# A two-layer decoder on one core: block-diagonal attention keys written by 16 loads per unit instead of a load and a multiplication by a mask of heads

## The chip, the cores and the metric

The kernel runs on one core of one Trainium2 chip. A core has TensorE (PE: matrix products), VectorE (DVE), ScalarE (ACT), GpSimd (POOL) and SyncE (SP), which here only issues DMA transfers. Each engine works through its own list of instructions in order; engines wait for each other by counting semaphores. The metric is the time of one execution on the device, in microseconds (us).

## What is computed

The input x has 16 batches of 512 positions of 256 numbers; the context has 16 batches of 64 positions. Six sublayers follow each other, each on a layer norm of x and added to x. Those the change touches are the two cross attentions (16 heads of 16 numbers, 64 keys):

```python
x = x + L0_attn(_layernorm(x), ...)       # gated recurrence along the positions
x = x + L0_xattn(_layernorm(x), ctx, ctx, mask, ...)
x = x + L0_ffn(_layernorm(x), ...)
x = x + L1_attn(_layernorm(x), ...)       # an LSTM of 20 units gives positions of attention
x = x + L1_xattn(_layernorm(x), ctx, ctx, fside, mask, ...)
x = x + L1_ffn(_layernorm(x), ...)        # one of 8 experts per position
...
Q = q @ Wq.T + bq; K = k @ Wk.T + bk; V = v @ Wv.T + bv      # each split into 16 heads
scores = einsum('bhqd,bhkd->bhqk', Q, K) / sqrt(d_head)      # masked keys: fill or -1e9
attn = softmax(scores); attn = attn * group_prob             # group_prob in layer 1 only
O = einsum('bhqk,bhkd->bhqd', attn, V) @ Wo.T + bo
```

## The kernel before

**Units and lanes.** Work is cut into units: four batches (GB = 4) by 128 positions. There are 16 units of layer 0 (first three sublayers) and 16 of layer 1. Two lanes run interleaved: lane 0 does 12 units of layer 0 and then 4 of layer 1, lane 1 does 4 of layer 0 and then 12 of layer 1. Tiles of lane 0 are called l0_..., of lane 1 l1_...

**Stages and bodies.** Seven stages follow each other. Stages 0 and 1 have two bodies each, with a unit of layer 0 in both lanes. Stages 2 and 3 have four bodies each, with a unit of layer 0 in lane 0 and one of layer 1 in lane 1. Stage 4 has four bodies with lane 1 alone, stage 5 two bodies with layer 1 in both lanes. The LSTM (names pg, gates, slots, uin) runs beside stages 1 to 4, 32 steps in a body of stages 2 to 4 and 64 in one of stage 1; each step goes TensorE, ScalarE, VectorE, ScalarE, VectorE. The experts run beside stages 4 and 5 and alone in stage 6.

**What sets the order.** `planned` (L343) lays out each stage by list scheduling: every step has an engine, a cost in us written by hand and the steps it needs (`attention_steps`, L202, for the attention). The resulting order per engine is what each engine's list holds; waits on semaphores keep it correct. In gaps over 0.3 us that the plan sees on TensorE it puts `warm` matrix products (L950), which nothing reads. A change of one step's cost or needs can move steps on all engines.

**The attention of a unit** has eight rounds u (batch b = u // 2, half of the heads j = u % 2). For each round TensorE forms the scores of 8 heads at once as one product of the queries with block-diagonal keys: rows 16e to 16e+15 of `kbd` hold the keys of head e in the columns of head e, and zeros elsewhere. Before the change:

- `load_context` (L726) on SyncE loads, for the lane's next unit, the values `vg`, the keys `kg` (one transfer of 256 KB) and the mask (and in layer 1 `gp`), once the previous unit's rounds are over (`pv` of round 7).
- the step `keys` (L1707) on GpSimd multiplies `kg`, repeated over 8 heads, by `headmask` into one of two buffers `kbd`, once for each round: 128 rows of 512 numbers. The buffer is free again when the scores of four rounds earlier are done.
- the step `score` (L900) on TensorE adds the mask's product (L907) and the product with `kbd` (L909); then come VectorE's maximum (L1395), ScalarE's exponentials (L1161), in layer 1 VectorE's sums (L1400) and GpSimd's gate (L1719), and the turn, the product with the values and VectorE's division (L1410).
- `neg` (L1387, L1390) on VectorE makes the additive mask, and `orow` (L1665 with rowO) on GpSimd adds the output bias to x, after the last `keys` of the unit.

**Other names.** L1348 to L1373 and L1450 are VectorE's part of a layer norm (statistics, shift, and the normalized x of batches 2 and 3; ScalarE does 0 and 1 in L1126); L1697 and L1691 are its reciprocal roots on GpSimd. L1665 with rowOut, rowF are other bias rows, L1677 copies LSTM inputs into `slots`, L1734 masks position weights, L1728, L1750 and L1755 are GpSimd's indexed transfers of the experts. L867 turns the normalized x on TensorE, L942 is the LSTM's product. L724 loads x for a unit of layer 0.

## Time and profile before

| | us |
|---|---|
| median of 3 runs | 2620.91 |
| lowest, highest | 2616.39, 2623.07 |
| the profiled execution, its own time | 2631.95 |
| its span, first to last instruction | 2629.8 |
| stages 0 and 1, from 84 | to 680 |
| stages 2 and 3 | 680 to 1823 |
| stages 4 and 5, then 6 | 1823 to 2560, to 2630 |

All rows come from one profiled execution. Groups of instructions give a count, the busy time of all of them, the mean of one in ns, and the idle time of the engine just before them with what ended it. In a timeline each row has a start and a duration, and idle time before it in brackets where there was some. The chain is the sequence of work and waits followed back from the last instruction.

### The profile page before, as it was taken

To read this page: it belongs to the slowest core of one execution; us is meant where nothing else is said; L and a number is where in the kernel's file an instruction comes from. 1 tells how busy PE (TensorE), PEld (TensorE's weight loads), DVE (VectorE), ACT (ScalarE), POOL (GpSimd) and SP (SyncE) were. 2 spreads that over 40 slices of the span, in tenths; PEclk is the share of its full clock that TensorE was granted. 3 is DMA by queue.
4 is the path that set the end of the run, shared out by engine and by line. 5 is a ranking of instruction groups with operands and counts; after the bars stand their busy time and mean duration, and the time that the engine had idled before them with its cause. 6 is when DMAs were issued, how large, how long until landed. Compare 5 with 4: busy or idle time off the path is not lost.

```text
span 2629.8 us, 42733 instructions
## 1 busy us (share of the span) xinstructions
PE 2302.6 (88%) x11585; PEld 1499.8 (57%) x11585; DVE 1578.0 (60%) x5494; ACT 1425.8 (54%) x5145; POOL 1046.3 (40%) x1124
## 2 busy tenths in 40 slices
PE   5799999999899898989898989798888878697887
PEld 2365655656556564747465655556655546566664
DVE  4456477676665766666576767676645646364541
ACT  1263646658464554737474747464655646465632
POOL 0223241232233433333334343433555545487665
PEclk9899999999899999989899999998999999798989
DMA  4302020100302011111203030302353243353323
GB/s 161 99 11 64 14 62 1 51 9 1 94 9 70 17 53 35 46 49 30 48 17 94 1 95 0 86 16 81 103 126 97 78 121 90 112 163 98 92 62 105
DMA packets 203923, 168.32 MB, mean 64 GB/s; under 512 B 56847, under 2 KB 196717, under 8 KB 203452
## 3 DMA queue, kind: packets, MB, share of 16 engines
q1 hardware_dynamic: 189372, 140.73, 18.6%
q0 software_dynamic: 14336, 25.28, 3.3%
q8 instruction: 67, 1.10, 0.2%
q14 instruction: 148, 1.21, 0.2%
HBM read 125.11 MB, written 53.40 MB: 68 GB/s over the span
## 4 chain that ended last, share of the span: by engine, by line
PE 37%; issue 24%; DVE 16%; POOL 12%; ACT 5%; SPq 3%; DMA 2%; POOLq 0%; DVEq 0%; another core or an unknown queue 0%; ACTq 0%
PE p L970 7%; PE p L950 4%; PE p L873 4%; PE p L933 3%; PE p L909 3%; POOL l_scratch L1719 3%; PE p L867 3%; PE p L884 2%; PE pg L942 2%; PE p L923 2%; DVE l_xnat L1450 2%; POOL l_kbd L1712 2%; POOL l_xres L1665 2%; DVE ln_stats L1348 1%; PE p L1023 1%
## 5 line engine op out<-in xcount | busy, mean ns | idle before, releaser
L1161 ACT ACTIVATE l_scratch<-p,l_mx 128x64 f32<-128x64 f32 x2048 | 483.4, 323 | 30.8 <-DVE l_mx L1395 20.2
L950 PE MATMUL p<-warm 128*128 128x512 bf16 x1802 | 476.1, 394 | 1.2 <-DVE l_sums L1343 1.2
L1712 POOL TENSOR_TENSOR l_kbd<-l_kg,headmask 128x512 f32<-128x512 f32 x256 | 264.1, 1044 | 385.0 <-PE p L909 289.6
L942 PEld LDWEIGHTS pg<-slots,wcat 128*128 128x128 f32 x1024 | 174.7, 197 | 287.6 <-DVE slots L1649 218.6
L1697 POOL TENSOR_TENSOR ln_rstd<-ln_ve,neghalf 128x4 f32<-128x4 f32 x96 | 98.2, 1022 | 547.2 <-DVE ln_ve L1357 545.1
L942 PE MATMUL pg<-slots,wcat 128*128 128x16 f32 x1024 | 180.9, 252 | 125.7 <-DVE slots L1649 105.0
L933 PEld LDWEIGHTS p<-l_vg,l_scratch 128*128 128x128 f32 x2048 | 254.4, 193 | 62.3 <-ACT l_scratch L1169 37.7
L950 PEld LDWEIGHTS p<-warm 128*128 128x128 bf16 x1802 | 185.4, 107 | 173.5 <-issue 40.0
L933 PE MATMUL p<-l_vg,l_scratch 128*128 128x34 f32 x2048 | 264.0, 276 | 6.8 <-ACT l_scratch L1169 4.5
L909 PE MATMUL p<-l_kbd,l_qT 128*128 128x512 f32 x512 | 265.4, 600 | 0.6 <-POOL l_kbd L1712 0.5
L1719 POOL TENSOR_TENSOR l_scratch<-l_scratch,gp 128x512 f32<-128x512 f32 x128 | 162.5, 1270 | 221.3 <-DVE l_sums L1400 219.8
L1395 DVE TENSOR_REDUCE l_mx<-p 128x8 f32<-128x512 f32 x256 | 176.2, 690 | 93.9 <-PE p L909 86.8
L1641 DVE SCALAR_TENSOR_TENSOR pg<-gates,pg 20x16 f32<-20x16 f32 x512 | 89.8, 175 | 214.0 <-ACT gates L1109 194.1
L1109 ACT ACTIVATE gates<-pg 96x16 f32<-96x16 f32 x512 | 92.0, 180 | 219.9 <-PE pg L942 208.3
L867 PE MATMUL p<-ident,l_xnat 128*128 128x128 f32 x1024 | 158.4, 291 | 40.1 <-ACT l_xnat L1126 36.6
L1169 ACT ACTIVATE l_scratch<-p 128x512 f32<-128x512 f32 x256 | 153.6, 600 | 52.7 <-PE p L923 44.8
L1113 ACT ACTIVATE pg<-pg 20x16 f32<-20x16 f32 x512 | 77.3, 151 | 191.0 <-DVE pg L1645 179.5
L923 PE MATMUL p<-ident,l_scratch 128*128 128x128 f32 x1024 | 159.0, 282 | 22.7 <-DVE l_xnat L1410 16.8
L867 PEld LDWEIGHTS p<-ident,l_xnat 128*128 128x128 f32 x1024 | 124.6, 151 | 85.6 <-ACT l_xnat L1126 65.1
L1126 ACT ACTIVATE l_xnat<-l_xres,ln_shift,ln_rstd 128x256 f32<-128x256 f32 x160 | 87.1, 592 | 154.9 <-DVE ln_shift L1373 153.7
L923 PEld LDWEIGHTS p<-ident,l_scratch 128*128 128x128 f32 x1024 | 120.8, 148 | 81.2 <-issue 40.5
L1649 DVE SCALAR_TENSOR_TENSOR slots<-gates,pg 20x16 f32<-20x16 f32 x528 | 88.8, 171 | 104.8 <-ACT pg L1113 93.0
(281 smaller groups left out, 4381.7 us busy)
## 6 DMA issues: line engine op xcount, KB each, us to landing
xln<-xln_dram SPq DMA_DIRECT2D x40, 512.0 KB, 4.7
l_vg<-v_dram SPq DMA_DIRECT2D x32, 544.0 KB
x_dram<-l_xres SPq DMA_DIRECT2D x32, 512.0 KB, 4.2
l_kg<-k_dram SPq DMA_DIRECT2D x32, 256.0 KB
xln_dram<-l_xnat SPq DMA_DIRECT2D x16, 512.0 KB, 3.0
l_xres<-x_dram SPq DMA_DIRECT2D x16, 512.0 KB
x_dram<-l_xnat SPq DMA_DIRECT2D x16, 512.0 KB
xin<-in_x SPq DMA_DIRECT2D x12, 512.0 KB, 3.8
```

Source lines behind the costliest of these rows:

```text
L867: i = pe.transpose(banks[l][m][:, b * P:(b + 1) * P], src[:, b, m * P:(m + 1) * P], ident[:, :])
L909: pe.matmul(banks[l][j], w.qT[:, j, b * P:(b + 1) * P], w.kbd[b % 2][:, j, :, :].rearrange("p a k -> p (a k)"), start=False, stop=True).th ...
L923: i = pe.transpose(t_bank[l][:, p * P:(p + 1) * P], src, ident[:, :])
L933: i = pe.matmul(o_of(l, layer, c)[:, q * VW:(q + 1) * VW], w.exT[:, j, p, :], w.vg[:, b, q * VW:(q + 1) * VW], start=True, stop=True)
L942: pe.matmul(pg[:, 0:B], wcat[:, :], slots[:, s % STEPS, :], start=True, stop=True).then_inc(l_pe, 1)
L950: pe.matmul(banks[1][0] if layer > NC_ else px, warm[:, 0:P], warm[:, :], start=True, stop=True)
L970: i = pe.matmul(bank, w[:, k, half * P:(half + 1) * P], tiles[lane].xT[:, k, :], start=(k == 0), stop=(k == NH - 1))
L1161: i = act.activation(w.ex[b % 2][:, NE * j + h, :], banks[lane][j][:, h * SK:(h + 1) * SK], ACT.Exp, scale=-1.0, bias=w.mx[:, u % 4, h:h + 1])
L1169: act.activation(w.exT[:, i_ % 2, :, :], t_bank[lane].rearrange("p (a t) -> p a t", a=4), ACT.Identity).then_inc(t.exT, 1)
L1395: dve.tensor_reduce(w.mx[:, u % 4, :], banks[l][j].rearrange("p (a k) -> p a k", a=NE), AX_X, ALU.min).then_inc(t.top, 1)
L1712: pool.tensor_tensor(w.kbd[b % 2][:, j, :, :], w.kg[:, j, b:b + 1, :].broadcast_to([P, NE, SK]), headmask[:, :].rearrange("p (a o) -> p a ...
L1719: pool.tensor_tensor(ex, ex, gp[lane][:, b:b + 1, :].broadcast_to([P, NE, SK]), ALU.mult).then_inc(t.gated, 1)
```

## The change

The product by the mask of heads is dropped: `kg`, `headmask` and the step `keys` are gone. `kbd` becomes one tile per lane with room for all four batches, [128, 4, 2, 8, 64], set to zero once at the program's start by VectorE. `load_context` then issues, instead of the one transfer of 256 KB, 16 transfers, one for each head block e and half h: 16 rows, 4 batches, 64 numbers each, straight into the blocks of the diagonal. The zeros around them stay. TensorE waits once per unit, in round 0, for all loads of the unit (17 or 18 transfers, constant LOADS), and no more for `kbd` in each round. `orow` is planned after `score` 3 and waits for it.

To make room, buffers of the experts are laid over the LSTM's inputs `R` (xgT, xh, xq, xy) and over the bias rows of layer 0 (one xg; the rows are now one tile rows0). The same instructions use them.

The plan of every stage is laid out anew without `keys`. It holds 1823 warm products where there were 1802.

```diff
+LOADS = (16 * (NE * NH + 1), 16 * (NE * NH + 2))
...
-        self.kg = sb(f"{name}_kg", [P, NH, GB, SK])
-        self.kbd = [sb(f"{name}_kbd{i}", [P, NH, NE, SK]) for i in range(2)]
+        self.kbd = sb(f"{name}_kbd", [P, GB, NH, NE, SK])
...
-            ("pool", "keys", u, 1.07, [("score", u - 4)]),
-            ("pe", "score", u, 1.1, [("qland", u % 2), ("keys", u), ("neg", 0), ("exp", 4 * (u - 2) + 3)]),
+            ("pe", "score", u, 1.1, [("qland", u % 2), ("neg", 0), ("exp", 4 * (u - 2) + 3)]),
...
-    steps += [("pool", "orow", 0, 2.3, [("keys", 7)])]
+    steps += [("pool", "orow", 0, 2.3, [("score", 3)])]
...
-        xg = tD + [sb(f"xg{i}", [P, 2 * D])[:, :] for i in range(2, TILE_SLOTS)]
+        xg = tD + [rows0[:, :, :].rearrange("p i d -> p (i d)")] + [sb(f"xg{i}", [P, 2 * D])[:, :] for i in range(3, TILE_SLOTS)]
...
-        xy = [sb(f"xy{i}", [P, D]) for i in range(OUT_SLOTS)]
+        xy = [R[:, i, P:3 * P] for i in range(OUT_SLOTS)]
...
-                    sp.wait_ge(t.kbd, 2 * GB * m)
+                    sp.wait_ge(t.scores, 2 * GB * m)
                     sp.wait_ge(t.pv, 2 * GB * m)
                     sp.wait_ge(t.neg, m)
...
-                sp.dma_start(w.kg[:, :, :, :], k_dram[layer, :, :, bass.ds(GB * g, GB), :]).then_inc(t.m_load, 16)
+                for e in range(NE):
+                    rows = slice(HD * e, HD * e + HD)
+                    for h in range(NH):
+                        sp.dma_start(w.kbd[rows, :, h, e, :], k_dram[layer, rows, h, bass.ds(GB * g, GB), :]).then_inc(t.m_load, 16)
...
-                    pe.wait_ge(t.kbd, N + 1)
+                    if u == 0:
+                        pe.wait_ge(t.m_load, LOADS[0] * n + LOADS[0] if layer == 0 else LOADS[0] * LAYER0_UNITS[l] + LOADS[1] * n + LOADS[1])
                     pe.matmul(banks[l][j], w.qT[:, j, b * P:(b + 1) * P],
-                              w.kbd[b % 2][:, j, :, :].rearrange("p a k -> p (a k)"), start=False, stop=True
+                              w.kbd[:, b, j, :, :].rearrange("p a k -> p (a k)"), start=False, stop=True
...
+            for t in tiles:
+                dve.memset(t.kbd[:, :, :, :, :], 0.0)
...
                 elif family == "orow":
+                    pool.wait_ge(t.scores, 2 * GB * m + 4)
                     add_row(lane, rowO[layer], t.base)
-                elif family == "keys":
-                    if i_ == 0:
-                        pool.wait_ge(t.m_load, 32 * n + 32 if layer == 0 else 32 * LAYER0_UNITS[lane] + 48 * n + 48)
-                    if positive(N - 3):
-                        pool.wait_ge(t.scores, N - 3)
-                    pool.tensor_tensor(
-                        w.kbd[b % 2][:, j, :, :], w.kg[:, j, b:b + 1, :].broadcast_to([P, NE, SK]),
-                        headmask[:, :].rearrange("p (a o) -> p a o", o=1).broadcast_to([P, NE, SK]), ALU.mult
-                    ).then_inc(t.kbd, 1)
```


**Where the order moves.** GpSimd, in the loop body of stage 2, from the bias row of lane 0's unit to the root of the position weights. Before:

```order
L1665 TENSOR_TENSOR l0_xres<-l0_xres,rowOut 128x1024
L1675 REGISTER_ALU
L1677 ISA
L1677 COPY slots<-R 96x128
L1712 TENSOR_TENSOR l0_kbd1<-l0_kg,headmask 128x512
L1712 TENSOR_TENSOR l1_kbd1<-l1_kg,headmask 128x512
L1712 TENSOR_TENSOR l0_kbd1<-l0_kg,headmask 128x512
L1687 ISA
L1688 TENSOR_TENSOR pos1_nrm<-pos1_nrm,neghalf 128x4
L1693 ISA
L1697 TENSOR_TENSOR ln1_rstd<-ln1_ve,neghalf 128x4
```

Now:

```order
L1669 TENSOR_TENSOR l0_xres<-l0_xres,rows0 128x1024
L1679 REGISTER_ALU
L1681 ISA
L1681 COPY slots<-R 96x128
L1691 ISA
L1692 TENSOR_TENSOR pos1_nrm<-pos1_nrm,neghalf 128x4
L1697 ISA
L1701 TENSOR_TENSOR ln1_rstd<-ln1_ve,neghalf 128x4
```

The three products into kbd between the copy into slots and the root are gone; the rest stands in the same order (line numbers are four higher).

TensorE at the same place, around the turn of lane 0's normalized x (l0_xnat) by ident. Before:

```order
L950 MATMUL p1<-warm 128x512 x2
L941 REGISTER_ALU
L942 MATMUL pg<-slots,wcat 128x16
L950 MATMUL p1<-warm 128x512 x11
L953 ISA
L867 MATMUL p0<-ident,l0_xnat 128x128 x4
L941 REGISTER_ALU
L942 MATMUL pg<-slots,wcat 128x16
L867 MATMUL p0<-ident,l0_xnat 128x128 x4
L950 MATMUL p1<-warm 128x512 x7
L1021 REGISTER_ALU
L1023 MATMUL p1<-xln1,l1_scratch 128x256 x4
```

Now:

```order
L952 MATMUL p1<-warm 128x512 x7
L943 REGISTER_ALU
L944 MATMUL pg<-slots,wcat 128x16
L955 ISA
L868 MATMUL p0<-ident,l0_xnat 128x128 x8
L952 MATMUL p1<-warm 128x512 x10
L963 ISA
L972 MATMUL p0<-l0_xT,wD 128x512
L943 REGISTER_ALU
L944 MATMUL pg<-slots,wcat 128x16
```

The LSTM's product (pg) that stood between the two halves of the turn now stands ahead of both or behind the first wD product. The 11 warm products between it and the turn are gone; 7 stand ahead of it where 2 did, and 10 follow the turn where 7 did.

SyncE's queue at the start of stage 0, first loads of both lanes. Before:

```order
L724 DMA xin<-in_x 128x4x256
L735 DMA l0_vg<-v_dram 128x4x272
L737 DMA l0_kg<-k_dram 128x2x256
L739 DMA mask8_0<-in_mask0 128x4x64
L724 DMA xln1<-in_x 128x4x256
L735 DMA l1_vg<-v_dram 128x4x272
L737 DMA l1_kg<-k_dram 128x2x256
L739 DMA mask8_1<-in_mask0 128x4x64
```

Now:

```order
L722 DMA xin<-in_x 128x4x256
L733 DMA l0_vg<-v_dram 128x4x272
L738 DMA l0_kbd<-k_dram 16x4x64 x16
L740 DMA mask8_0<-in_mask0 128x4x64
L722 DMA xln1<-in_x 128x4x256
L733 DMA l1_vg<-v_dram 128x4x272
L738 DMA l1_kbd<-k_dram 16x4x64 x16
L740 DMA mask8_1<-in_mask0 128x4x64
```

Lane 1's x (xln1) now stands behind 16 key transfers of lane 0 and not behind one.

## Rows read from the trace of the kernel before

**Rows 1.** The page's first part: busy us, share of the span, instructions, by engine

```profile
PE 2302.6 (88%) x11585; PEld 1499.8 (57%) x11585; DVE 1578.0 (60%) x5494; ACT 1425.8 (54%) x5145; POOL 1046.3 (40%) x1124
```

**Rows 2.** The chain that ended last: shares of the span by engine, by line

```profile
PE 37%; issue 24%; DVE 16%; POOL 12%; ACT 5%; SPq 3%; DMA 2%; POOLq 0%; DVEq 0%; another core or an unknown queue 0%; ACTq 0%
...
by line: issue 24.1%; PE p L970 7.0%; PE p L950 3.8%; PE p L873 3.6%; PE p L933 3.5%; PE p L909 3.3%; POOL l_scratch L1719 2.9%; PE p L867 2.7%; PE p L884 2.4%; PE pg L942 2.1%; PE p L923 2.1%; DVE l_xnat L1450 2.0%; POOL l_kbd L1712 1.6%; 
```

**Rows 3.** Groups by line and shape: count, busy us, mean ns, idle before

```profile
L950 PE MATMUL p<-warm 128*128 128x512 bf16 x1802 | 476.1, 394 | 1.2 <-DVE l_sums L1343 1.2
...
L909 PE MATMUL p<-l_kbd,l_qT 128*128 128x512 f32 x512 | 265.4, 600 | 0.6 <-POOL l_kbd L1712 0.5
...
L1712 POOL TENSOR_TENSOR l_kbd<-l_kg,headmask 128x512 f32<-128x512 f32 x256 | 264.1, 1044 | 385.0 <-PE p L909 289.6 <-DMA mask<-in_mask 95.2
```

**Rows 4.** The same view, VectorE's normalizing operation from two sources

```profile
L1450 DVE TENSOR_SCALAR l_xnat<-l_xres,ln_mv,ln_rstd 128x256 f32<-128x256 f32 x160 | 63.0, 436 | 2.0
...
L1450 DVE TENSOR_SCALAR l_xnat<-xin,ln_mv,ln_tmp 128x256 f32<-128x256 f32 x24 | 51.4, 2183 | 1.0
```

**Rows 5.** Timeline (start us, us), GpSimd, start of a body of stage 2

```profile
980.80 2.03 POOL L1712 TENSOR_TENSOR l_kbd<-l_kg,headmask 128x512 f32<-128x512 f32 x2
...
1002.21 2.36 POOL L1665 TENSOR_TENSOR l_xres<-l_xres,rowOut 128x1024 f32<-128x1024 f32 x1
...
1004.93 3.04 POOL L1712 TENSOR_TENSOR l_kbd<-l_kg,headmask 128x512 f32<-128x512 f32 x3
```

**Rows 6.** Timeline, VectorE, the same place; last row the like of L1373 elsewhere

```profile
980.18 2.68 DVE L1373 SCALAR_TENSOR_TENSOR ln_shift<-ln_mv,ln_rstd 128x4 f32<-128x4 f32 x1 [3.63 <-POOL ln_rstd L1697]
...
997.98 0.97 DVE L1364 TENSOR_TENSOR ln_tmp<-ln_tmp,ln_mv 128x4 f32<-128x4 f32 x1
...
1001.30 0.97 DVE L1373 SCALAR_TENSOR_TENSOR ln_shift<-ln_mv,ln_tmp 128x4 f32<-128x4 f32 x1
...
1002.40 5.72 DVE L1450 TENSOR_SCALAR l_xnat<-xin,ln_mv,ln_tmp 128x256 f32<-128x256 f32 x2
...
689.00 0.17 DVE L1373 SCALAR_TENSOR_TENSOR ln_shift<-ln_mv,ln_rstd 128x4 f32<-128x4 f32 x1
```

**Rows 7.** Timeline, TensorE, the same place

```profile
1009.16 0.60 PE L942 MATMUL pg<-slots,wcat 128*128 128x16 f32 x2 [4.34 <-DVE slots L1649]
```

**Rows 8.** Window: us; PE, PEld, DVE, ACT, POOL busy us; clock, DMA, GB/s

```profile
980.00:1123.00 143.00, 128.59 (x638) 82.36 (x638) 92.41 (x317) 80.41 (x301) 50.49 (x47) 0.95 0.15 40
```

**Rows 9.** Timeline, all engines, start of stage 0

```profile
85.50 0.62 SPq L737 DMA_DIRECT2D l_kg<-k_dram  x1
...
86.83 0.55 SPq L724 DMA_DIRECT2D xln<-in_x  x1
...
93.04 0.75 DVE L1348 BATCH_NORM_STATS2 ln_stats<-xln 128x6 f32<-128x256 f32 x2 [9.99 <-DMA xln<-in_x]
...
95.61 2.04 POOL L1712 TENSOR_TENSOR l_kbd<-l_kg,headmask 128x512 f32<-128x512 f32 x2 [95.17 <-DMA mask<-in_mask]
```

**Rows 10.** Timeline, key loads on SyncE's queue, VectorE's step that needs them

```profile
951.52 0.53 SPq L737 DMA_DIRECT2D l_kg<-k_dram  x1
...
996.51 0.29 DVE L1387 TENSOR_SCALAR l_neg<-mask 128x256 bf16<-128x256 uint8 x1
...
676.57 1.81 SPq L737 DMA_DIRECT2D l_kg<-k_dram  x1
```

**Rows 11.** Timeline, GpSimd, second body of stage 5

```profile
2410.51 5.03 POOL L1712 TENSOR_TENSOR l_kbd<-l_kg,headmask 128x512 f32<-128x512 f32 x5
...
2415.51 1.25 POOL L1734 TENSOR_TENSOR l_scratch<-l_scratch,below 128x512 f32<-128x512 f32 x1
```

**Rows 12.** Timeline, preparation at the program's start

```profile
8.81 5.18 DVE L1270 MEMSET R<- 64x6144 f32 x1 [1.32 <-issue]
...
22.56 0.70 SPq L702 DMA_DIRECT2D wcat<-in_c_gatesel  x1
...
28.52 0.61 DVE L1281 TENSOR_SCALAR wA<-wA,normw 128x256 f32<-128x256 f32 x2 [12.39 <-DMA wms<-in_W_mu_sig]
```

More of the change, by code:

```diff
@@ L151, in __init__ @@
     def __init__(self, name, sem):
-        self.turns, self.lands, self.kbd = sem(f"{name}_turns"), sem(f"{name}_lands"), sem(f"{name}_kbd")
+        self.turns, self.lands = sem(f"{name}_turns"), sem(f"{name}_lands")
         self.scores, self.top = sem(f"{name}_scores"), sem(f"{name}_top")
@@ L519, in decoder_program @@
         same = sb("same", [P, P], BF16)
-        headmask = sb("headmask", [P, NE])
         rank = sb("rank", [P, NE])
@@ L549, in decoder_program @@
         biasG = sb("biasG", [96, 2])
-        rowOut = sb("rowOut", [P, D])
+        rows0 = sb("rows0", [P, 2, D])
+        rowOut, rowF = rows0[:, 0, :], rows0[:, 1, :]
         rowO = [sb(f"rowO{l}", [P, D]) for l in range(2)]
-        rowF = sb("rowF", [P, D])
         ones = sb("ones", [P, 1])
@@ L595, in decoder_program @@
         xw += parts(xin[0].rearrange("p b d -> p (b d)"))
-        xg = tD + [sb(f"xg{i}", [P, 2 * D])[:, :] for i in range(2, TILE_SLOTS)]
+        xg = tD + [rows0[:, :, :].rearrange("p i d -> p (i d)")] + [sb(f"xg{i}", [P, 2 * D])[:, :] for i in range(3, TILE_SLOTS)]
         xid = [sb(f"xid{i}", [P, 2], I32) for i in range(TILE_SLOTS)]
-        xgT = [sb(f"xgT{i}", [P, D]) for i in range(2)]
-        xh = [sb(f"xh{i}", [P, P]) for i in range(2)]
-        xq = [sb(f"xq{i}", [P, P]) for i in range(2)]
-        xy = [sb(f"xy{i}", [P, D]) for i in range(OUT_SLOTS)]
+        xgT = [R[:, OUT_SLOTS + i, P:3 * P] for i in range(2)]
+        xh = [R[:, 8, (1 + i) * P:(2 + i) * P] for i in range(2)]
+        xq = [R[:, 9, (1 + i) * P:(2 + i) * P] for i in range(2)]
+        xy = [R[:, i, P:3 * P] for i in range(OUT_SLOTS)]
         ctxA = xln[1][:, :, :, :].rearrange("p i b d -> p (i b d)").rearrange("p (h b k) -> p h b k", h=NH, b=B)
@@ L657, in decoder_program @@
         loads = [
-            (ident[:, :], a["c_ident"]), (tri[:, :], a["c_tri"]), (headmask[:, :], a["c_headmask"]),
+            (ident[:, :], a["c_ident"]), (tri[:, :], a["c_tri"]),
             (rank[:, :], a["c_rank"]), (posl, a["c_posl"]),
@@ L1265, in _ @@
             dve.memset(warm[:, :], 1.0)
+            for t in tiles:
+                dve.memset(t.kbd[:, :, :, :, :], 0.0)
             dve.memset(carry[:, :, :], 0.0)
-            for t in xg[2:]:
+            for t in xg[3:]:
                 dve.memset(t, 0.0)
@@ L1385, in attention_step @@
                     if layer == 0:
-                        dve.wait_ge(t.m_load, 32 * n + 32)
+                        dve.wait_ge(t.m_load, LOADS[0] * n + LOADS[0])
                         dve.tensor_scalar(w.neg[:, :, :], mask8[l][:, :, :], 1.0, -FMAX, ALU.subtract, ALU.mult).then_inc(t.neg, 1)
                     else:
-                        dve.wait_ge(t.m_load, 32 * LAYER0_UNITS[l] + 48 * n + 48)
+                        dve.wait_ge(t.m_load, LOADS[0] * LAYER0_UNITS[l] + LOADS[1] * n + LOADS[1])
                         dve.tensor_scalar(w.neg[:, :, :], mask32[l][:, :, :], 1.0, -1e9, ALU.subtract, ALU.mult).then_inc(t.neg, 1)
```

## The prediction

> **What bounds the kernel now.** I read the engine shares first. TensorE is busy 88% of the span, GpSimd 40% [rows 1]. But TensorE's figure holds 1802 warm products, 476.1 us, which nothing reads [rows 3]; no engine is full, and the time is made of what waits for what. The chain says so: TensorE is 37% of it, unexplained issue time 24%, VectorE 16%, GpSimd 12% [rows 2]. The products by the mask of heads are 256 of 1044 ns, 264.1 us of GpSimd, and yet they are on the chain for 1.6% of the span, 42 us [rows 2, 3]. TensorE waited for them only 0.5 us in all [rows 3]. As a supplier of TensorE, then, the removed step is early nearly everywhere.
>
> The second thing to see is what it does to VectorE. Normalizing one 128x256 block takes VectorE 436 ns on average when the source is the residual (160 times) and 2183 ns when it is freshly loaded x (24 times, lane 0's 12 units) [rows 4]. Shape, type and engine are the same. The timeline gives the reason: the two blocks that start at 1002.40 take 5.72 us together and end at 1008.12, just after GpSimd's three products into kbd end at 1007.97; a bias row and a copy into slots fill GpSimd before these [rows 5, 6]. At 980.18 an operation on four numbers per row takes 2.68 us, where its like takes 0.17, and ends with the pair of products that ends at 982.83 [rows 5, 6]. So VectorE's operations between SBUF tiles stand still while GpSimd works. This happens at the seam between two bodies, where TensorE has little else: it then waits 4.34 us for the LSTM's `slots`, which VectorE can write only after the held blocks [rows 7]. This is what the change can give back. That TensorE is busy for 128.59 of the 143 us of such a body [rows 8] bounds it: over 14 us a body can't be won without moving warm products.
>
> The Trainium skill (SBUF — State Buffer, "SBUF: two separate sides") describes a port pair that VectorE and GpSimd share as an exclusive lock: one "fully blocks" while the other holds it for a whole instruction. The trace agrees in form. By that rule the held time vanishes wherever the products vanish, and the first term below would be taken whole (58 us) and not at 45.
>
> **The change, part by part.** Sums are made against the profiled execution's own 2631.95 us, which is 11.04 above the median of 2620.91; I scale by their ratio at the end.
>
> *VectorE held, stages 2 and 3.* In the body shown: the operation at 980.18 is held from 980.80 to 982.83 by the products, 2.68 − 0.17 − 0.6 (copies into slots before them) = 1.9. Two small operations of 0.97 us each at 997.98 and 1001.30 (0.17 without) save 0.8 each, 1.6. The two blocks end at 1008.12; with nothing behind the copy, which ends at 1004.93, the second block needs about 0.4 more and ends near 1005.4: 2.7. Sum 6.2 us [rows 5, 6]. That body is a bad one: averaged over all 12 units the two blocks are held 2 × (2.183 − 0.436) = 3.5 us, here 5.72 − 0.87 = 4.85, a ratio of 0.72 [rows 4, 6]. Eight bodies × 6.2 × 0.75 = 37 us. The rest of the 6.2 I leave with what is next late: the bias row of 2.36 us stays in front of the same blocks [rows 5].
>
> *Stages 0 and 1*, four bodies: no row of mine shows their seam, only the mean over all units [rows 4]. I take a third of the 6.2, 2 us each: 8.
>
> *GpSimd itself late.* In the second body of stage 5, five products (5.03 us) stand between the indexed transfers and the masking of position weights, which starts the moment they end, 2415.51 [rows 11]: 5 us. At the start of stage 0 two products wait for lane 1's mask load and end at 97.65, ahead of the first root [rows 9]: 2 us, counted below. Of the remaining 35 us that the products have on the chain [rows 2] most lies in the rounds, where TensorE is nearly full; TensorE's 0.5 us of waiting [rows 3] says nothing is won there, the chain says all. I take a quarter, 9, and keep 0 and 35 for the range.
>
> *The 16 transfers.* SyncE took 0.53 us to issue the single key load in the usual case and 1.81 in the worst [rows 10]. A transfer of 64 pieces has no row. It could cost less than the 0.53 or as much as the 1.81; I take 0.5 with its gap, since 0.53 belongs to the same tensors and the same queue: 8 us per unit, 7.4 more than now, 512 transfers in all. What hides it: both lanes' loads of a seam are issued from 951 on and their mask is first used by `neg` at 996.51 [rows 10]. With 16 us in place of 1 they are done by about 970. Behind them in the queue stand stores of the finished unit and, at the turn of stages 1 and 2, the load of x3: a few us late, with consumers later still. 2 us for all.
>
> *The start.* There the cover is gone. Lane 1's x was issued at 86.83 and its statistics began at 93.04, after the x had come; now it is issued 7.4 us later [rows 9]. TensorE's first work hangs on lane 1. Landing may be quicker, since less is queued with it: statistics at 98 rather than 93.0, +5. Against this the first root no longer waits for the products: they end at 97.65, and statistics begun at 93.04 take a little over 2, so it waited about 2.4. +2 in all with rounding, bounds −1 and +7.
>
> *Preparation.* Zeroing R took 5.18 us for 6144 numbers, so 4096 numbers twice take 6.9, less one dropped buffer, 0.4. VectorE idled 12.39 us up to 28.52, that is from 16.13; it now finishes at 22.6, when the queue reaches the late loads that wait for it, which started at 22.56 [rows 12] and come 0.4 earlier without headmask's load. Nothing; 0.5 if I am off.
>
> *Order.* 21 warm products more, at 476.1 / 1802 = 0.26 us [rows 3], are 5.5 us if on the path and 0 if not: 3. At the seam TensorE no longer has the LSTM's product between the halves of lane 0's turn, which is where it waited 4.34 us [rows 7]; this helps, but elsewhere the new plan may place a step badly. I count 0 and ±15 us for the range.
>
> Sum: 37 + 8 + 5 + 9 − 2 − 2 − 3 = 52 us. 2631.95 − 52 = 2580; times 2620.91 / 2631.95 is **2569 us**.
>
> **Rivals.** *(a) More comes back.* All held time (8 × 6.2 + 8 = 58) and all 42 us of the chain, and the clock: TensorE's granted clock is 0.95 of full in that body [rows 8], 7 us of 143, part of it lost right after the idle time of the seam. 58 + 42 − 7 = 93, with some clock 100: 2520. For it: the blocks end with GpSimd's work to within 0.15 us. Against: the bias row stays, TensorE is dense in the rounds.
>
> *(b) Nothing comes back.* The seam is then bound by the LSTM or by the warm products, and the held time only turns into another wait. The three costs, 7 us, and a few us won in stage 5 stay: 2620. Against it: TensorE waits for `slots` there by name [rows 7].
>
> *(c) SyncE's queue becomes the bound, slower.* Both lanes load in the same stretch; from 952 to `neg` at 996.51 there are 44 us, of which 2 are a landing. 32 transfers fit if one takes under 42 / 32 = 1.3 us. At the worst row, 1.81 and a gap of 0.05 [rows 10], they take 59.5 us, 17 too many, in each of the 12 bodies of stages 0 to 3: 2620 + 200 = 2820. The Trainium skill (DMA: Bandwidth & Descriptors, "Rules for kernel authors") speaks for such a case: coalesce small transfers, under 64 KB they are mostly overhead, and these are 16 KB. With its fixed 2.0 us each, one after another, 32 would be an estimated 64 us, past the point too. The trace speaks against it: 256 KB were issued in 0.53 us in the usual case, and lane 0's mask was there for `neg`, which ran without a wait [rows 10].
>
> *(d) The new plan is worse* by the 15 us of its range, with half of the gains: near 2612; by more, or where the start costs 7: over 2629, slower.
>
> **How the numbers follow.** Forecast 0.60; (a) 0.17; (b) 0.10; (c) 0.05; (d) 0.08, half of it slower. About 0.3%, 8 us, is what a measurement of this kernel can tell from no change. Faster: 0.60 + 0.17 + a part of (d) and (b), 0.82; same: 0.09; slower: (c) and half of (d), 0.09. The range reaches from (a), 2520, to 2624, where (b) is held: left out are (c), the slow part of (d) and what lies under 2520.
>
> **What would show it.** The blocks of L1450 on fresh x: from 2183 ns to about 1300 (the bias row stays). VectorE's busy time down by some 60 us, GpSimd's by 264. TensorE's wait for `slots` at the seam near 1 us. Bodies of stages 2 and 3 shorter by about 5 us each, those of stage 4 by under 3. Key transfers of about 0.5 us on SyncE, `neg` never waiting after stage 0; lane 1's first statistics near 98. The forecast is wrong if these transfers take over 1.3 us, if bodies of stages 2 and 3 do not shorten while L1450 does, or if waits for `slots` appear elsewhere.

## The result: half of the gain was forecast

| | us | against before |
|---|---|---|
| before, median of 4 runs | 2618.65 | |
| changed, median of 4 runs (2511.10 to 2523.76) | 2520.59 | ratio 0.9608, 95% interval 0.9568 to 0.9648 |
| the change again, beside other runs of before, twice | | 0.9614 (0.9592 to 0.9636); 0.9603 (0.9576 to 0.9629) |

The kernel became 3.9% faster, 102 us. I had forecast 52 us and put this outcome, 2520, down as rival (a). Medians of before lay between 2614 and 2639 us from one set of runs to the next, so experiments are compared by their ratio to the runs of before in their own set; 0.001 is 2.6 us. One execution of the changed kernel took 5751 us, far off all the others, and is left out of its ratio.

The profiled execution of the changed kernel took 2511.1 us, span 2508.9. Its page begins:

```profile
PE 2274.1 (91%) x11606; PEld 1488.8 (59%) x11606; DVE 1464.7 (58%) x5495; ACT 1418.2 (57%) x5145; POOL 786.9 (31%) x868
```

Against [rows 1] GpSimd lost 259 us, which is the removed work. VectorE lost 113 us although the change only adds to its work (6.9 us of zeroing): this is time for which its operations had been stretched. I had said 60. The groups by line and shape (count, busy us, mean ns, idle before and what ended it), to be held against [rows 3, 4] and against these two of before:

```profile
L942 PE MATMUL pg<-slots,wcat 128*128 128x16 f32 x1024 | 180.9, 252 | 125.7 <-DVE slots L1649 105.0 <-POOL slots L1677 18.1 <-issue 0.5
...
L1390 DVE TENSOR_SCALAR l_neg<-mask 128x256 bf16<-128x256 int32 x16 | 14.1, 890 | 5.9 <-issue 5.7
```

And of the changed kernel:

```profile
L952 PE MATMUL p<-warm 128*128 128x512 bf16 x1823 | 474.2, 393 | 1.2 <-DVE l_sums L1347 1.2
...
L944 PE MATMUL pg<-slots,wcat 128*128 128x16 f32 x1024 | 178.6, 250 | 73.5 <-DVE slots L1653 57.1 <-POOL slots L1681 13.6 <-issue 0.3
...
L1454 DVE TENSOR_SCALAR l_xnat<-xin,ln_mv,ln_tmp 128x256 f32<-128x256 f32 x24 | 16.9, 747 | 0.8
...
L1394 DVE TENSOR_SCALAR l_neg<-mask 128x256 bf16<-128x256 int32 x16 | 5.4, 346 | 7.0 <-issue 6.7
```

The blocks of fresh x went from 2183 ns to 747, `neg` on the int32 mask from 890 to 346, and TensorE's idle time ahead of the LSTM's products from 125.7 us to 73.5. The timelines of VectorE and GpSimd at the seam of [rows 5, 6], now at 966:

```profile
965.87 0.29 DVE L1391 TENSOR_SCALAR l_neg<-mask 128x256 bf16<-128x256 uint8 x1
966.23 0.16 DVE L1462 TENSOR_TENSOR ln_tmp<-ln_rstd 128x4 f32<-128x4 f32 x1
966.43 0.16 DVE L1377 SCALAR_TENSOR_TENSOR ln_shift<-ln_mv,ln_tmp 128x4 f32<-128x4 f32 x1
966.62 0.17 DVE L1653 SCALAR_TENSOR_TENSOR slots<-gates,pg 20x16 f32<-20x16 f32 x1
966.84 0.73 DVE L1454 TENSOR_SCALAR l_xnat<-xin,ln_mv,ln_tmp 128x256 f32<-128x256 f32 x2
```

```profile
963.62 1.26 POOL L1730 TENSOR_TENSOR l_scratch<-l_scratch,below 128x512 f32<-128x512 f32 x1 [3.52 <-ACT l_scratch L1211]
965.18 1.02 POOL L1695 TENSOR_TENSOR ln_rstd<-ln_ve,neghalf 128x4 f32<-128x4 f32 x1 [0.30 <-DVE ln_tmp L1372]
970.75 2.36 POOL L1669 TENSOR_TENSOR l_xres<-l_xres,rows 128x1024 f32<-128x1024 f32 x1 [4.55 <-ACT l_xres L1138]
```

The two blocks took 0.73 us together where they took 5.72. The row of bias, which I had left in front of them, now starts 3 us after their end. `slots` is written at 966.62 ahead of the blocks, so that TensorE's wait of 4.34 us [rows 7] is gone here. Another wait for `slots` stays, two LSTM products earlier: 3.76 us before, 6.42 now.

```profile
996.54 0.60 PE L942 MATMUL pg<-slots,wcat 128*128 128x16 f32 x2 [3.76 <-DVE slots L1649]
```

```profile
963.57 0.61 PE L944 MATMUL pg<-slots,wcat 128*128 128x16 f32 x2 [6.42 <-DVE slots L1653]
```

Where the 121 us between the two profiled spans went. The lengths of the stages in us are taken between like instructions: the first block of fresh x of stages 0, 2 and 3, then lane 1's `neg` at the first body of stages 4 and 5 and at the second body of stage 5. The last column holds this second body and stage 6. Three executions of the changed kernel:

| | start | stages 0, 1 | stage 2 | stage 3 | stage 4 | stage 5, first body | rest |
|---|---|---|---|---|---|---|---|
| before | 109.2 | 595.4 | 580.2 | 545.8 | 423.8 | 153.3 | 222.2 |
| changed | 107.5 | 587.0 | 533.8 | 516.0 | 396.2 | 156.6 | 211.8 |
| changed, 2nd | 108.5 | 585.6 | 529.3 | 519.2 | 406.6 | 169.2 | 213.5 |
| changed, 3rd | 108.9 | 586.6 | 530.1 | 516.4 | 406.4 | 169.8 | 210.4 |
| product kept | 119.0 | 595.4 | 581.6 | 548.5 | 428.4 | 152.8 | 222.3 |
| power instead | 116.5 | 586.5 | 545.3 | 514.0 | 413.0 | 166.4 | 220.2 |
| nothing, order of before | 108.3 | 586.8 | 539.7 | 512.1 | 423.7 | 166.3 | 219.8 |

Up to stage 3 executions agree within 5 us; stage 4 and the first body of stage 5 of one kernel differ by 10 to 13, and nothing under that is read there. The last three rows are experiments of the next section.

### The profile page after: what moved, and what is told of

It reads as the page before. It is cut to its first block and busy times, and to the rows that moved or that the text cites. A ratio compares the mean times of both kernels' runs of the same rounds, so it can differ in the third digit from the quotient of the medians.

```text
span 2508.9 us, 42915 instructions
## 1 busy us (share of the span) xinstructions
PE 2274.1 (91%) x11606; PEld 1488.8 (59%) x11606; DVE 1464.7 (58%) x5495; ACT 1418.2 (57%) x5145; POOL 786.9 (31%) x868
## 5 line engine op out<-in xcount | busy, mean ns | idle before, releaser
L911 PE MATMUL p<-l_kbd,l_qT 128*128 128x512 f32 x512 | 262.4, 594 | 0.0
L944 PE MATMUL pg<-slots,wcat 128*128 128x16 f32 x1024 | 178.6, 250 | 73.5 <-DVE slots L1653 57.1
L1146 ACT ACTIVATE l_xT<-p 128x512 f32<-128x512 f32 x192 | 108.2, 596 | 58.4 <-PE p L868 56.2
```

Of the source, the lines that this page charges most:

```text
L911: pe.matmul(banks[l][j], w.qT[:, j, b * P:(b + 1) * P], w.kbd[:, b, j, :, :].rearrange("p a k -> p (a k)"), start=False, stop=True).then_i ...
L944: pe.matmul(pg[:, 0:B], wcat[:, :], slots[:, s % STEPS, :], start=True, stop=True).then_inc(l_pe, 1)
L1146: act.activation(w.xT[:, h, :], banks[lane][h], ACT.Identity).then_inc(ln[lane].landed, 1)
```

## The experiments

### Taking the change apart: order, queue, hold

Three kernels in one set, all with the 16 transfers, all planned as before (the planner still sees the keys' steps). They differ in what GpSimd does at the 256 places:

```
-            ("pe", "score", u, 1.1, [("qland", u % 2), ("neg", 0), ("exp", 4 * (u - 2) + 3)]),
+            ("pool", "keys", u, 1.07, [("score", u - 4)]),
+            ("pe", "score", u, 1.1, [("qland", u % 2), ("keys", u), ("neg", 0), ("exp", 4 * (u - 2) + 3)]),
...
-    steps += [("pool", "orow", 0, 2.3, [("score", 3)])]
+    steps += [("pool", "orow", 0, 2.3, [("keys", 7)])]
```

**Nothing there**: the step issues no instruction.

> The changed kernel (16 transfers, no product), but planned as before: the planner still sees the steps of the keys with their 1.07 us and their needs, and nothing is issued for them. So the order on TensorE, VectorE and ScalarE and the 1802 warm products are those of the kernel before. Theory A (the products themselves cost the time, by holding VectorE or by standing in GpSimd's queue): most of the gain is here, 2520 to 2535 us. Theory B (the new order brought a large part of it): 2560 to 2580 us.

Measured: 0.9649 (0.9618 to 0.9681).

**The product kept:**

```
+                    pool.tensor_tensor(
+                        w.kbd[:, b, j, :, :], w.kbd[:, b, j, :, :],
+                        headmask[:, :].rearrange("p (a o) -> p a o", o=1).broadcast_to([P, NE, SK]), ALU.mult
+                    ).then_inc(t.kbd, 1)
```

> Keys by the 16 transfers, planned as before, and the product by the mask of heads is done all the same, in place on the block-diagonal keys (128x512 f32, same size, same places in GpSimd's order, TensorE waits for it as before). Only the single load, the order of waits on it and the source of the product differ from the kernel before. Theory A: everything comes back, 2610 to 2630 us. Theory C (the gain came from loads that land elsewhere, or from keys that are in place early): about 2530 us. If the transfers cost SyncE's queue anything, it shows here as time above 2620.

Measured: 1.0047 (1.0027 to 1.0066).

**A power in its place:**

```
+                    pool.tensor_tensor(idle[:, 1 + lane, :], idle[:, 0, :], neghalf[:, :], ALU.pow).then_inc(t.kbd, 1)
```

> As the kernel with the product kept, but at each of its 256 places GpSimd does a power of 128x4 numbers, which takes 1.02 us (ln_rstd in the page) against 1.04 of the product and moves 4 numbers a row instead of 512. GpSimd's queue is as long as before; if the small operation does not hold VectorE, the hold is gone. Theory A1 (VectorE was held): 2530 to 2550 us. Theory A2 (steps queued behind the products on GpSimd came late): 2600 to 2620 us. My sum had 45 us for the first and 14 for the second of 52, so by its shares about 2560 of the measured gain of 98.

Measured: 0.9703 (0.9675 to 0.9731).

Read from before to changed in steps of 2620 us: the 16 transfers +12; product to power −90; power to nothing −14; order of before to the new one −11 (0.9649 to the mean of three, 0.9608). The last two are known to about ±11 us (both intervals of a difference, 0.003 each, added as squares) and barely differ from zero. The first two are plain. But the start has a large share in two of the four, as the first column of the table shows. With the transfers and the product kept it is 10 us longer than before (119.0 for 109.2), with nothing in the product's place 8 us shorter than with the power (108.3 for 116.5). At the start GpSimd's first keys wait for lane 1's mask, which now comes behind the key transfers, and the first root stands behind them: they began at 105.46 where they had begun at 95.61 [rows 9], and VectorE waited 6.55 us for the root.

```profile
105.46 2.03 POOL L1719 TENSOR_TENSOR l_kbd<-l_kbd,headmask 128x512 f32<-128x512 f32 x2 [105.02 <-DMA mask<-in_mask]
```

```profile
108.54 1.01 DVE L1368 TENSOR_TENSOR ln_tmp<-ln_rstd 128x4 f32<-128x4 f32 x1 [6.55 <-POOL ln_rstd L1703]
```

The changed kernel has no such wait, so the +12 is no measure of what the transfers cost it, and of the −14 only some 6 us are GpSimd's lateness elsewhere.

The timelines show why the third kernel is so fast, with GpSimd just as busy. Product kept, GpSimd and VectorE:

```profile
1007.10 2.04 POOL L1719 TENSOR_TENSOR l_kbd<-l_kbd,headmask 128x512 f32<-128x512 f32 x2
1009.10 2.36 POOL L1671 TENSOR_TENSOR l_xres<-l_xres,rows 128x1024 f32<-128x1024 f32 x1
1011.39 0.46 POOL L1683 COPY slots<-R 96x128 f32 x1
1011.82 3.03 POOL L1719 TENSOR_TENSOR l_kbd<-l_kbd,headmask 128x512 f32<-128x512 f32 x3
```

```profile
1008.19 0.97 DVE L1379 SCALAR_TENSOR_TENSOR ln_shift<-ln_mv,ln_tmp 128x4 f32<-128x4 f32 x1
1009.29 5.72 DVE L1456 TENSOR_SCALAR l_xnat<-xin,ln_mv,ln_tmp 128x256 f32<-128x256 f32 x2
```

Power instead, the same place:

```profile
982.22 1.98 POOL L1722 TENSOR_TENSOR idle<-idle,neghalf 128x4 f32<-128x4 f32 x2
984.17 2.36 POOL L1672 TENSOR_TENSOR l_xres<-l_xres,rows 128x1024 f32<-128x1024 f32 x1
```

```profile
982.59 0.16 DVE L1380 SCALAR_TENSOR_TENSOR ln_shift<-ln_mv,ln_tmp 128x4 f32<-128x4 f32 x1
982.89 0.74 DVE L1457 TENSOR_SCALAR l_xnat<-xin,ln_mv,ln_tmp 128x256 f32<-128x256 f32 x2
```

Two powers of 0.99 us each lie over VectorE's operations and do not stretch them; two products hold an operation on four numbers from 0.16 to 0.97. And the row of bias, in both, starts right behind. With the products VectorE is late and meets it; with the powers it is done 0.5 us before it comes. One hold pushes VectorE into the next: that is what my account by single operations missed. The lock that the Trainium skill describes (SBUF — State Buffer, "SBUF: two separate sides") is what the trace shows for the wide products, 5.72 us where 0.74 are needed; under the powers no run here shows it.

### Which products: those at the seam

Eight products stand in each unit. The first four need no score and run at the seam, the last four among the rounds. Two kernels keep the product for one half and have the power for the other (the second has `i_ >= 4`):

```
+                    if i_ < 4:
+                        pool.tensor_tensor(
+                            w.kbd[:, b, j, :, :], w.kbd[:, b, j, :, :],
...
+                    else:
+                        pool.tensor_tensor(idle[:, 1 + lane, :], idle[:, 0, :], neghalf[:, :], ALU.pow).then_inc(t.kbd, 1)
```

> Planned as before; of the eight keys of a unit the first four have the product of 128x512 (these stand at the seam, ahead of the attention), the last four the power of 128x4. All eight products gave 1.0047 of before, all eight powers 0.9703, 90 us apart. Theory A1 (the hold of VectorE at the seam is what costs): most of the 90 us are here, ratio 0.995 to 1.005. Theory A3 (holds anywhere cost alike): half of it, 0.987.

> The counterpart: power for the first four keys of a unit, product for the last four, which run among the rounds. Theory A1: near 0.972 to 0.977. Theory A3: 0.987. The two together also show whether the parts add up: 90 us in all if they do, less or more if each hold hides or worsens the other's.

Measured: first four 0.9987 (0.9966 to 1.0008), last four 0.9726 (0.9699 to 0.9753). All products stood at 1.0047, none at 0.9703 (another set): of these 0.034 the first four alone bring 0.028, the last four alone 0.002. The products at the seam, then, are the cause of 74 of the 90 us. The first four alone stretched the blocks of fresh x to 2183 ns, exactly as all eight did; the last four left them at 636:

```profile
L1458 DVE TENSOR_SCALAR l_xnat<-xin,ln_mv,ln_tmp 128x256 f32<-128x256 f32 x24 | 51.4, 2183 | 1.0
```

```profile
L1458 DVE TENSOR_SCALAR l_xnat<-xin,ln_mv,ln_tmp 128x256 f32<-128x256 f32 x24 | 14.3, 636 | 1.0
```

### The clock alone

One kernel is the changed one without the 771 warm products of stages 2 and 3:

```
-IDLE, FILL, WARM = 0.3, 0.9, (0, 1, 2, 3, 4, 6)
+IDLE, FILL, WARM = 0.3, 0.9, (0, 1, 4, 6)
```

> The changed kernel without the 771 warm products of stages 2 and 3 (they are read by nothing). Nothing holds VectorE more than before: only TensorE idles more, so the granted clock falls. It prices the clock alone. Theory (a part of the 90 us is the clock, 43 us less at half clock in stage 2): the time at half clock in stages 2 and 3 rises from 65 us to over 300 and the time by a quarter to a half of the rise, 2570 to 2650 us. If the clock matters little in these stages, or the warm products stand in the way of real work: 2520 us or less.

Measured: 0.9923 (0.9899 to 0.9946), 31 thousandths over the changed kernel, 83 us. The windows of stage 2 (length; PE, PEld, DVE, ACT, POOL busy us; granted clock, DMA, GB/s) of before, product kept, power instead, changed, and this one:

```profile
705.00:1285.00 580.00, 521.74 (x2573) 335.72 (x2573) 370.30 (x1277) 322.11 (x1206) 203.03 (x185) 0.94 0.15 40
```

```profile
714.00:1296.00 582.00, 520.98 (x2540) 335.95 (x2575) 370.81 (x1279) 321.76 (x1207) 203.22 (x185) 0.93 0.15 40
```

```profile
703.00:1248.00 545.00, 507.86 (x2538) 330.69 (x2573) 336.76 (x1275) 321.28 (x1206) 200.63 (x185) 0.96 0.16 43
```

```profile
695.00:1228.00 533.00, 499.38 (x2562) 325.43 (x2562) 332.22 (x1274) 320.14 (x1205) 138.05 (x120) 0.97 0.18 44
```

```profile
696.00:1272.00 576.00, 465.78 (x2108) 333.53 (x2108) 332.47 (x1279) 321.89 (x1209) 138.22 (x120) 0.82 0.16 41
```

The clock has two levels, 2.4 and 1.2 GHz, so the time at the lower is 2 × (1 − mean) × length: 576 × 0.36 = 207 us without warm products, 533 × 0.06 = 32 with them. Those 175 us more cost 43 us in length, 0.25 us each, net of the time that the warm products themselves had taken. VectorE's busy time is 332 in both, so no hold separates them. By that price the fall from product (582 × 0.14 = 81) to power (545 × 0.08 = 44) is 37 × 0.25 = 9 us of the 37 by which stage 2 became shorter. The other 28 is the hold itself: in the trace of before, instruction by instruction, what VectorE's operations took over the fastest of their shape while a product ran, and on the chain of waits, sums to some 28 us in stage 2 and 27 in stage 3. So the gain of these two stages, 71 us from product to power, is 55 of held time and some 15 of clock. The estimate by one price is rough; without the warm products the low clock also lies under other work. And the sum closes better than it should: the holds by rows of bias that lie on the chain fell too from product to power, by some 5 us in each of these stages, and it leaves them out. That the products' hold is the larger part is shown; the split to the microsecond is not.

### What a transfer costs

> The changed kernel with one transfer of the same 256 KB per unit in place of 16. It puts the keys in the wrong places (the scores are not the reference's), to price the 16 transfers alone. As predicted (2 us of start and 2 of queue, at most 7 at the start): 2512 to 2520 us, no difference that can be told but lane 1's first statistics some 5 us earlier. If the 16 transfers cost much in SyncE's queue or the DMA engines: 2490 us or less.

```
-                for e in range(NE):
-                    rows = slice(HD * e, HD * e + HD)
-                    for h in range(NH):
-                        sp.dma_start(w.kbd[rows, :, h, e, :], k_dram[layer, rows, h, bass.ds(GB * g, GB), :]).then_inc(t.m_load, 16)
+                sp.dma_start(w.kbd[:, 0, 0, :, :].rearrange("p (h b) k -> p h b k", h=NH), k_dram[layer, :, :, bass.ds(GB * g, GB), :]).then_inc(t.m_load, 16)
```

Measured: 0.9542 (0.9509 to 0.9574), 17 us under the changed kernel and not 4. SyncE's queue at the start of the changed kernel:

```profile
84.56 7.69 SPq L738 DMA_DIRECT2D l_kbd<-k_dram  x16
92.29 0.43 SPq L740 DMA_DIRECT2D mask<-in_mask  x1
92.76 0.51 SPq L722 DMA_DIRECT2D xln<-in_x  x1
```

One transfer of 16 KB takes 0.48 us of the queue, as supposed. The first block of fresh x stood at 107.5 in the changed kernel and at 102.1 with one transfer: 5 us are here. Several kernels went after them.

**x of both lanes first**, then keys:

```
             for lane in range(2):
                 load_x(lane, 0, lane, 0)
+            for lane in range(2):
                 load_context(lane, 0, 0, lane, 0)
```

> The changed kernel with SyncE's first loads in another order: x of both lanes, then the two sets of 16 key transfers, so that lane 1's x no longer stands behind 7.7 us of key transfers. One transfer per unit brought the first block of x forward by 5.4 us. If that is the same delay: the first normalization 4 to 7 us earlier and 2513 us where the changed kernel gives 2520, ratio 0.9588. If the masks or the keys then come late for the first attention: no difference.

Measured in three sets: 0.9548 (0.9528 to 0.9567), 0.9569 (0.9545 to 0.9593), 0.9597 (0.9571 to 0.9624); beside the second the changed kernel stood at 0.9603. The mean of the three, 0.9571, is 10 us under that of the changed kernel, 0.9608; within the one set that has both, the intervals overlap.

> The kernel with x of both lanes loaded before the keys, again. If its 15 us were real: 0.954 to 0.956, 0.006 under the changed kernel of this set. If only the 3 us that its trace shows at the start are real: 0.002 under it at most.

**Eight transfers of 32 KB** (k_dram laid out so that both halves of the features lie together):

```
-                    for h in range(NH):
-                        sp.dma_start(w.kbd[rows, :, h, e, :], k_dram[layer, rows, h, bass.ds(GB * g, GB), :]).then_inc(t.m_load, 16)
+                    sp.dma_start(w.kbd[rows, :, :, e, :], k_dram[layer, rows, bass.ds(GB * g, GB), :, :]).then_inc(t.m_load, 16)
```

> As the one with x first, and the keys are stored so that both halves of the features come with one transfer: 8 of 32 KB per unit in place of 16 of 16 KB. If SyncE's queue costs only at the start, no difference from x first, ratio 0.9585 to 0.959; if the length of the queue costs in the bodies too (one transfer per unit gave 0.9542, of which the start explains 5 of 18 us), half of the rest comes back: 0.956.

Measured: 0.9569 (0.9552 to 0.9585), no better than x first beside it (0.9548). Its preparation stored the keys in more transfers and reached the first load of x at 91.90 us, where x first did at 83.16; the first block of fresh x stood at 108.0 for 104.4, which is 4 of the 5 us between the two. From that block to the end the two are equal (2391 and 2390 us): in the bodies eight transfers gained nothing.

**One transfer, with x first:**

> As x first, with one key transfer per unit of the same bytes (keys in the wrong places). What it gains over x first of this set is the price of the 16 transfers in the bodies: predicted 2 us, that is nothing that can be told; if the 18 us of the one-transfer kernel lay in the bodies, 0.005 under x first.

Measured: 0.9511 (0.9487 to 0.9536), 0.0058 under x first in the same set: 15 us. With x first and 16 transfers VectorE's first statistics began at 89.46 and it stood anyway, 7.66 us:

```profile
104.53 0.50 DVE L1392 TENSOR_SCALAR l_neg<-mask 128x256 bf16<-128x256 uint8 x2 [7.66 <-DMA mask<-in_mask]
```

The step `neg` of both lanes comes ahead of the first blocks, and its semaphore counted the 32 key transfers too. So the last experiment gave the keys a semaphore of their own and loaded mask, v, keys in this order:

```
-                        sp.dma_start(w.kbd[rows, :, h, e, :], k_dram[layer, rows, h, bass.ds(GB * g, GB), :]).then_inc(t.m_load, 16)
+                        sp.dma_start(w.kbd[rows, :, h, e, :], k_dram[layer, rows, h, bass.ds(GB * g, GB), :]).then_inc(t.k_load, 16)
...
+                        pe.wait_ge(t.k_load, 16 * NE * NH * (m + 1))
```

> As x first; mask, v and keys are loaded in this order, and the keys count on a semaphore of their own that only TensorE's first score waits for, so that VectorE's step on the mask no longer waits for the 32 key transfers of the start. If the mask was the wait: the first normalization of x at 100 to 102 us in place of 105.3 and 4 us less, ratio 0.0015 under x first. If in the bodies too something waited for the keys through the mask: up to 10 us less, 0.004. If TensorE then waits for the keys: no difference.

Measured: 0.9566 (0.9546 to 0.9585), x first beside it 0.9597 (0.9571 to 0.9624): 8 us, with intervals that overlap. The trace shows what was expected of the start, 102.0 in place of 105.3:

```profile
98.66 0.48 DVE L1393 TENSOR_SCALAR l_neg<-mask 128x256 bf16<-128x256 uint8 x2
99.42 2.31 DVE L1464 TENSOR_TENSOR ln_tmp<-ln_rstd 128x4 f32<-128x4 f32 x1 [0.27 <-POOL ln_rstd L1697]
101.96 0.73 DVE L1456 TENSOR_SCALAR l_xnat<-xin,ln_mv,ln_tmp 128x256 f32<-128x256 f32 x2
```

Of the 15 us that the 16 transfers cost even with x first, then, 3 to 5 are at the start. With one transfer stages 3 and 4 were shorter by 4 and 6 us too, which is no more than executions of one kernel differ by there. Where the other 10 us lie stays open.

### The other wide operation of GpSimd

64 rows of bias of 2.36 us stay, and stretch VectorE's operations by 27 us in the changed kernel (the excess over the fastest of each shape while a row runs). Three kernels: the addition cut to 4 numbers of a block (biases missing); the first row of a unit made to wait until VectorE has done its blocks; and the row added by TensorE.

```
-                pool.tensor_tensor(w.xres[:, :, :], w.xres[:, :, :],
-                                   row[:, :].rearrange("p (o d) -> p o d", o=1).broadcast_to([P, GB, D]),
-                                   ALU.add).then_inc(done, 1)
+                pool.tensor_tensor(w.xres[:, 0, 0:4], w.xres[:, 0, 0:4], row[:, 0:4], ALU.add).then_inc(done, 1)
```

> The changed kernel with the other large operation of GpSimd cut: the rows of bias are added to 4 numbers of a block instead of 1024 (64 operations of 2.36 us become short ones; the missing biases change the output). In the trace of the changed kernel they lengthen VectorE's operations by some 27 us. If a microsecond of VectorE held at the seam costs about 1.2 us of time, as the products did (90 us for 77 held), this gives 2510 - 32 = 2478 us and less time at half clock; if after the change TensorE's queue is the bound, nothing, 2505 to 2512.

Measured: 0.9524 (0.9502 to 0.9545), the changed kernel beside it 0.9614: 24 us. That is the hold together with 137 us less in GpSimd's queue; the two were not taken apart. In the profiled execution the gain lies in stage 3, 503.7 us where the changed kernel took 516 to 519.

> As x first, and the first row of bias of a unit (brow, 2.36 us on GpSimd) additionally waits until VectorE has normalized its blocks of x, so that it doesn't hold them; nothing is taken out. In the trace of the changed kernel these rows hold the blocks of x 4 times, 7.9 us, and small operations ahead of them 3 times, 5.0 us. If the hold is the cause: VectorE's operations held by rows of bias fall from 25 us to 15 and the time by 5 to 12 us, ratio 0.951 to 0.953. If the row now is late for x1: no difference or slower.

```
                     pool.wait_ge(l0.base_ready, n + 1)
+                    pool.wait_ge(s.normed_dve, s.before(0, n, 0) + 1)
```

Measured: 0.9572 (0.955 to 0.9594), x first beside it 0.9569: nothing. The rows' held time fell from 25 us to 20: the three holds of blocks in stage 3, 5.9 us, went, and stage 3 is as long as before, 516.0 us for 516.3. So these holds were off the path; in the trace of the changed kernel none of the operations that a row stretches lies on the chain. A held microsecond is not by itself a lost one: with the products gone VectorE has slack there.

> As the eight transfers, and GpSimd's 64 additions of a row of bias (2.36 us each, they hold VectorE for 27 us) are gone: TensorE adds the row by one product of one row of ones with the row, 128x512, ahead of each half of a projection, 128 of 0.6 us. Leaving the rows out gave 0.9524 where the changed kernel gave 0.9614, 24 us. If TensorE's 77 us find room where warm products stood, 20 us under the eight transfers, 0.949; if TensorE is the bound where they stand (its busy share is 91%), they cost what the hold gave: no difference, or slower by 10 us.

```
+                if b % 2 == 0:
+                    pe.matmul(pairs[l][:, b * D:(b + 2) * D], tri[0:1, :],
+                              row[0:1, :].rearrange("p (o d) -> p o d", o=1).broadcast_to([1, 2, D]), start=True, stop=False)
```

Measured: 0.9985 (0.9969 to 1.0001), with eight transfers beside it at 0.9569: 109 us slower, far worse than both cases of the expectation. Windows of stages 0 and 1, this kernel and the changed one:

```profile
103.00:735.00 632.00, 619.91 (x2809) 369.92 (x2807) 352.69 (x1364) 347.71 (x1212) 45.23 (x58) 0.99 0.11 33
```

```profile
107.00:694.00 587.00, 573.12 (x2740) 359.58 (x2738) 358.46 (x1362) 345.88 (x1209) 100.08 (x80) 0.99 0.12 35
```

TensorE was busy for 573 of 587 us there already; 47 us more made the stages 45 us longer. Stages 2 and 3, 40 and 21 us longer than with the eight transfers (570.2 for 530.2, 536.2 for 515.6), make up most of the rest. The row's product also costs twice what I had written: in the trace a f32 product of 512 columns stands as two matmuls (L911: 512 for 256 scores), so 128 became 256, 145 us for 77:

Warm products did not give way: they fell from 474 us to 442 in all, so that 113 of the 145 us came on top.

```profile
L954 PE MATMUL p<-warm 128*128 128x512 bf16 x1680 | 442.0, 394 | 1.2 <-DVE l_sums L1349 1.2
...
L873 PE MATMUL p<-rows,tri 1*128 1x512 f32 x128 | 73.6, 655 | 1.8 <-DVE l_qT L1497 1.3
L873 PE MATMUL p<-rowO,tri 1*128 1x512 f32 x128 | 71.9, 641 | 3.3 <-ACT l_xT L1152 2.9 <-issue 0.3
```

## Point by point

- **VectorE held, stages 2 and 3: 37 us forecast, 71 measured** from product to power. This is the step that failed, in its factor of 0.75. The 6.2 us of one seam were read rightly, but I called that body a bad one and scaled it down by the ratio of the mean over all 12 units [rows 4]. That mean has the four units of stages 0 and 1 in it, which I then counted a second time as a term of their own. The timeline of before shows two kinds of seam and nothing between: 1.42 us for the two blocks in each of the four units of stages 0 and 1, 5.71 to 5.75 in each of the eight of stages 2 and 3.

```profile
109.18 1.42 DVE L1450 TENSOR_SCALAR l_xnat<-xin,ln_mv,ln_tmp 128x256 f32<-128x256 f32 x2
...
704.58 5.74 DVE L1450 TENSOR_SCALAR l_xnat<-xin,ln_mv,ln_tmp 128x256 f32<-128x256 f32 x2
```

Without the factor the term is 50 us. The account also looked at one group of operations and its neighbours: `neg` on an int32 mask, 890 ns on average before and 346 now, was not in it. The whole held time on the chain in these stages is 55 us, 6.9 a body. And the clock, some 15 us, was put at nothing in the sum and stood in rival (a) only, though [rows 8] show 0.95.
- **The bias row "stays in front of the same blocks"**: wrong. It was in front of them because the products had made them late. 2183 ns went to 747 and not to 1300.
- **Stages 0 and 1: 8 forecast, 9 measured** (595.4 to 586.5).
- **GpSimd itself late**, 9 from the chain and 5 in stage 5: power to nothing gave 14 ± 11 over all, but 8 of these lie at the start, in a wait that the kernel before did not have. In the second body of stage 5, which I had named, the masking of position weights began 7.91 us after lane 1's `neg` before and 2.4 to 2.7 after it now, the 5 us that I said, and the body, to the end of its routing, took 135 to 139 us for 144.5. How much of that is the masking is not shown: with nothing in the product's place it began as early, at 2.9, and the body took 140.5; with the power it began as late as before and the body took 141.8. The first body did not become shorter in any execution (153.3 before, 156.6 to 169.8 after). Its windows show the clock: 0.89 before and in the first execution after, 0.84 in the second. Why the clock falls there is open.
- **The 16 transfers, 4 us**: 0.48 us each as taken, and `neg` waits for nothing after stage 0, as said. The price is 15 us with x first and 17 without, by the kernels with one transfer; some 10 us of it have no place yet. I counted the issue and asked for the first wait; the shared semaphore of mask and keys I had not followed.
- **The start: +2 us** forecast, −1.7 to −0.3 measured. Lane 1's statistics began at 96.89, where I had said 98, and the root no longer waited for products.
- **Order: −3 us for the warm products, 0 ± 15**: −11 ± 11. Not to be told from the forecast.
- **Stage 4, under 3 us a body**: 4 to 7 in three executions, of which product to power is 4 (15 us over the stage, little more than executions of one kernel differ by). I had no term for it; the products' holds on the chain of before sum to 7 us there.
- **TensorE's wait for `slots` at the seam "near 1 us"**: wrong. The wait of 4.34 us went, but the one ahead of it is 6.42.
- **The rivals.** (a) happened, by its mechanism: its 58 us of held time are 55 + 9, its clock is there; its 42 us of the chain were 14 at most. (b) falls with 0.9608. (c), a queue that becomes the bound, has the sign of the transfers' price and a thirteenth of its 200 us: 0.48 us each lie under its limit of 1.3. To coalesce small transfers, as the Trainium skill says (DMA: Bandwidth & Descriptors, "Rules for kernel authors"), brought 15 us with one in place of 16; with eight in place of 16 no gain showed. (d) did not occur.
- **The range** ended at 2520 because I placed rival (a) there as an end. 0.9608 of 2620.91 is 2518.

The two kernels that do all the work and beat both are the one with x first, 0.9571 as the mean of three sets, and the one with x and the masks first, 0.9566, about 10 us under the changed kernel.

## To carry to other kernels

Where VectorE's operations of one shape have two durations, sum the excess over the fastest of each shape for the whole stage, and take whole what of it lies on the chain: a hold that makes an engine late drives it into the next one, and the idle time behind it costs clock. Read every seam before you scale one by a mean. Warm products on a busy TensorE are no reserve; look at the window of the stage before moving work there. When one load becomes sixteen, follow every semaphore that counts them, not only their consumer.

## Unexpected of the hardware

- A power of 128x4 on GpSimd takes 1.02 us and a product of 128x512 1.04, yet only the second stretches VectorE's operations. Counting what they took over the fastest of their shape, as far as it lies under such an operation, it is 88 us in all under the products of before and 3 under the powers.
- A microsecond at half clock cost 0.25 us of length in stage 2, where TensorE was busy for 499 of 533 us.
- 47 us more of TensorE in stages 0 and 1 cost 45 us, though GpSimd's load more than halved there, from 100 to 45 us.
